# Feed-forward stages of a fused transformer kernel: output bias and parked rows added by GpSimd, shifted rows loaded two groups ahead, statistics taken two groups ahead

## The reference

```python
def _layer(x, wqkv, qs, ksc, wo, lg, lb, w1, b1, w2, b2):
    h = shift_token(x)          # second half of the channels comes from the token before
    ...                         # local attention with 8 heads of 64
    x = x + o @ wo
    h = shift_token(x)
    mu = h.mean(-1, keepdims=True)
    var = h.var(-1, keepdims=True)
    h = (h - mu) / jnp.sqrt(var + 1e-05) * lg + lb
    h = h @ w1 + b1
    a, g = jnp.split(h, 2, axis=-1)      # 341 and 341
    h = a * jax.nn.gelu(g, approximate=False)
    x = x + h @ w2 + b2
    return x
```

## Time and profile before

| what | value |
|---|---|
| median of the runs | 3533.75 us |
| the profiled execution's own time | 3536.04 us |
| its span, first to last instruction | 3534.4 us |
| mean granted TensorE clock | 0.947 of full speed |
| PE busy | 87% of the span |
| DVE busy | 76% |
| ACT busy | 46% |
| POOL busy | 24% |

### The profile page before, as it was taken

The page is one execution under the profiler, slowest core; times in us unless marked ns, Lnnn a source line. Parts: engine busy times, 40 slices in busy tenths (PEclk is TensorE's granted clock), DMA queues, the critical chain, the costliest instruction groups (busy, mean ns, idle before and its releaser), DMA issues. The chain is left out here.

```text
span 3534.4 us, 95348 instructions
## 1 busy us (share of the span) xinstructions
PE 3087.3 (87%) x34384; PEld 2089.7 (59%) x34384; DVE 2690.6 (76%) x5841; ACT 1625.1 (46%) x2545; POOL 839.8 (24%) x892
## 2 busy tenths in 40 slices
PE   4998769998999979999899668898979788888787
PEld 2666656665666656666566446666655456656545
DVE  5887767886777767766688779999956689989655
ACT  2665115664333335543466435555532355555422
POOL 1000000000000000001000156666611466666311
PEclk9999559998999989999899879999999999999999
DMA  4110001110000021110111100000001000000022
GB/s 137 30 29 20 0 5 31 29 29 4 0 0 0 0 44 38 41 22 1 28 27 29 62 13 7 9 9 8 4 19 27 13 11 10 9 11 8 19 65 59
DMA packets 193061, 80.16 MB, mean 23 GB/s; under 512 B 179124, under 2 KB 181864, under 8 KB 192232
## 3 DMA queue, kind: packets, MB, share of 16 engines
q1 hardware_dynamic: 191592, 73.25, 8.9%
q0 software_dynamic: 1280, 4.20, 0.3%
HBM read 35.58 MB, written 8.39 MB: 12 GB/s over the span
## 5 line engine op out<-in xcount | busy, mean ns | idle before, releaser
L770 ACT ACTIVATE probs_t<-ps_pt 128x1024 f32<-128x1024 f32 x256 | 262.2, 1024 | 384.8 <-PE ps_pt L884 384.8
L632 DVE TENSOR_REDUCE row_max<-ps_s 128x16 f32<-128x1024 f32 x256 | 313.2, 1224 | 135.2 <-PE ps_s L873 132.5
L1961 POOL TENSOR_TENSOR kblk<-kblk 128x1024 f32<-128x1024 f32 x128 | 301.6, 2356 | 199.1 <-DVE kblk L2002 199.1
L637 DVE TENSOR_TENSOR probs<-ps_s,row_max 128x1024 f32<-128x1024 f32 x256 | 312.1, 1219 | 11.7
L906 PE MATMUL ps_o<-v,probs_t 128*64 128x18 f32 x8192 | 285.4, 212 | 5.4 <-issue 5.2
L616 POOL TENSOR_TENSOR x<-x,out_bias_L 128x512 f32 (+1 forms) x32 | 40.7, 1272 | 1030.3 <-DVE x_norm L426 520.8
L906 PEld LDWEIGHTS ps_o<-v,probs_t 128*64 128x64 f32 x8192 | 260.1, 138 | 40.3 <-issue 19.0
L884 PE MATMUL ps_pt<-ident,probs 128*128 128x128 f32 x2048 | 277.1, 278 | 2.9 <-ACT probs L765 2.9
L873 PE MATMUL ps_s<-kblk,q_t 64*64 64x512 f32 x2048 | 273.5, 607 | 7.0 <-issue 6.9
L765 ACT ACTIVATE probs<-probs 128x1024 f32<-128x1024 f32 x256 | 269.6, 1053 | 16.6 <-DVE probs L637 15.1
L1979 POOL TENSOR_TENSOR kblk<-kblk,small_d 128x1024 f32<-128x1024 f32 x128 | 243.6, 1903 | 50.7 <-POOL small_d L1971 50.7
(11 more groups left out here) (307 smaller groups left out, 6930.7 us busy)
## 6 DMA issues: line engine op xcount, KB each, us to landing
ci<-in_ctx_t SPq DMA_DIRECT2D x64, 256.0 KB, 3.0
kblk<-k_t SPq DMA_DIRECT2D x768, 16.0 KB
ci<-x SPq DMA_DIRECT2D x64, 128.0 KB
ci<-x SPq DMA_DIRECT2D x128, 63.0 KB
x<-in_x_in SPq DMA_DIRECT2D x4, 1024.0 KB, 8.0
mask<-in_mask_l SPq DMA_DIRECT2D x64, 64.0 KB, 2.5
kblk<-ci SPq DMA_DIRECT2D x256, 16.0 KB
out<-x SPq DMA_DIRECT2D x1, 4096.0 KB, 11.1
```

Of the source, the lines that this page charges most:

```text
L632: dve.tensor_reduce(row_max[u % 2][:, :], scores_of(u), AX, ALU.max).then_inc(max_ready.sem, 1)
L637: dve.tensor_tensor(probs[u % 2][:, :, :], scores_of(u), row_max[u % 2][:, :].unsqueeze(2).broadcast_to([P, HEADS, S]), ALU.subtract).then ...
L770: act.activation(probs_t[:, :, :], ps_pt[:, :, :].rearrange("p a (r t) -> p (a r) t", t=P), ACT.Copy).then_inc(pt_ready.sem, 1)
L1961: pool.tensor_tensor(a, a, b_, ALU.add).then_inc(rotated.sem, 1)
```

## The change

The bias matmuls are taken out of PE's program. `b_dn` is loaded as full rows, and POOL adds it to the rows of x (`add_bias`) once the shifted copies of these rows are there; in layer 1 POOL adds the parked rows too, in place of DVE. SP loads the shifted rows two groups ahead, in `local_attention` too, and fetches the parked rows under a semaphore of their own (`fetched`). DVE takes the statistics of group g+2 between gates 0 and 1 of group g and their variances behind gate 2, and normalises group g+1 ahead of gate 0. The loops are `run_pipeline`, which was there before: it calls the body from group -2 on, and `has(g)` says whether there is such a group.

```diff
-                           (b_dn[l][0:1, :], w["b_dn"][l]), (ln_gb[l][:, :], w["ln"][l])]
+                           (b_dn[l][:, :], w["b_dn"][l]), (ln_gb[l][:, :], w["ln"][l])]
...
-                sp.wait_ge(zeroed.sem, len(row_bias) + 3 + DEPTH)
+                sp.wait_ge(zeroed.sem, len(row_bias) + 3)
...
-                for l in range(DEPTH):
-                    dve.memset(b_dn[l][:, :], 0.0).then_inc(zeroed.sem, 1)
...
-                if last:
-                    sp.dma_start(parked[par], out[:, rows, :]).then_inc(shift_loaded.sem, 16)
-
-            def body(g, par, ahead):
-                if ahead:
+
+            def fetch(g, par):
+                sp.dma_start(parked[par], out[:, bass.ds(g * GT, GT), :]).then_inc(fetched.sem, 16)
+
+            def body(g, par):
+                if not has(g + 2):
+                    return
+                if has(g):
                     sp.wait_ge(xt_in_psum.sem, xt_in_psum.at(g, 1))
                     sp.sem_inc(sp_turn.sem, 1)
-                    load(g + 1, 1 - par)
+                wait_past(sp, shift_loaded, g + 1, shift_loaded.per if has(g + 1) else 0)
+                sp.sem_inc(sp_turn.sem, 1)
+                load(g + 2, par)
+                if last:
+                    if has(g):
+                        sp.wait_ge(biased.sem, biased.at(g, biased.per))
+                        sp.sem_inc(sp_turn.sem, 1)
+                    wait_past(sp, fetched, g + 1, 16 if has(g + 1) else 0)
+                    sp.sem_inc(sp_turn.sem, 1)
+                    fetch(g + 2, par)
 
             sp.wait_ge(first_rows.sem, 4)
-            load(0, 0)
-            run_groups(sp, body)
+            run_pipeline(sp, body, 2)
...
-            shift_loaded.opens(4 * 16 if last else 3 * 16)
+            shift_loaded.opens(3 * 16)
+            fetched.opens(16 if last else 0)
+            biased.opens(2 if last else 1)
...
-                                pe.matmul(ps_o[:, u * P:(u + 1) * P], wide[c][0:m, u * P:(u + 1) * P],
-                                          w_dn[l][0:m, c, :], start=c == 0 and u == 0, stop=False,
-                                          skip_group_check=True)
-                        for u in range(GT):
-                            last = pe.matmul(ps_o[:, u * P:(u + 1) * P], ones[:, :], b_dn[l][:, :], start=False,
-                                             stop=True, skip_group_check=True)
+                                last = pe.matmul(ps_o[:, u * P:(u + 1) * P], wide[c][0:m, u * P:(u + 1) * P],
+                                                 w_dn[l][0:m, c, :], start=c == 0 and u == 0, stop=c == NC - 1,
+                                                 skip_group_check=True)
                         last.then_inc(y_done.sem, 1)
...
-                    def body(g, par, ahead):
-                        if ahead:
-                            root(pool, g + 1)
+                    def add_bias(g, par):
+                        if has(g + 1):
+                            pool.wait_ge(x_norm_ready.sem, x_norm_ready.at(g + 1, GT))
+                            pool.sem_inc(pool_turn.sem, 1)
+                        pool.wait_ge(shift_loaded.sem, shift_loaded.at(g, 48))
+                        pool.sem_inc(pool_turn.sem, 1)
+                        rows = x[:, bass.ds(g * GT, GT), :]
+                        pool.tensor_tensor(rows, rows, b_dn[l][:, :].unsqueeze(1).broadcast_to([P, GT, P]), ALU.add)\
+                            .then_inc(biased.sem, 1)
                         if last:
+                            pool.wait_ge(biased.sem, biased.at(g, 1))
+                            pool.sem_inc(pool_turn.sem, 1)
+                            pool.wait_ge(fetched.sem, fetched.at(g, 16))
+                            pool.sem_inc(pool_turn.sem, 1)
+                            pool.tensor_tensor(rows, rows, parked[par], ALU.add).then_inc(biased.sem, 1)
+
+                    def body(g, par):
+                        if has(g):
+                            add_bias(g, par)
+                        if has(g + 2):
+                            root(pool, g + 2)
+                        if last and has(g):
                             pool.wait_ge(added.sem, added.at(g, 1))
                             pool.sem_inc(pool_turn.sem, 1)
                             rows = bass.ds(g * GT, GT)
                             pool.dma_start(out[:, rows, :], x[:, rows, :]).then_inc(result_out.sem, 16)
 
-                    root(pool, 0)
-                    run_groups(pool, body)
+                    run_pipeline(pool, body, 2)
                     if last:
                         pool.wait_ge(result_out.sem, 16 * GROUPS)
 
                 @block.vector
                 def _(dve):
-                    def body(g, par, ahead):
-                        if ahead:
-                            dve.wait_ge(shift_loaded.sem, shift_loaded.at(g + 1, shift_loaded.per))
-                            norm_stats(dve, g + 1, hi[1 - par])
-                        flat = window_of(g)
-                        if last:
-                            dve.tensor_tensor(flat, flat, parked[par].rearrange("p u c -> p (u c)"), ALU.add)\
-                               .then_inc(unparked.sem, 1)
-                        for c, (at, m) in enumerate(HC):
-                            dve.wait_ge(a_in_psum.sem, a_in_psum.at(g, c + 1))
-                            dve.wait_ge(gelu_done.sem, gelu_done.at(g, c + 1))
-                            dve.wait_ge(y_done.sem, y_done.at(g, 0))
-                            dve.scalar_tensor_tensor(out=wide[c][0:m, :], in0=bank_a[c % 2][0:m, :],
-                                                     scalar=b_up1[l][0:m, c:c + 1], in1=wide[3 + c][0:m, :],
-                                                     op0=ALU.add, op1=ALU.mult).then_inc(gated.sem, 1)
-                            if ahead and c == 0:
-                                normalise(dve, g + 1, hi[1 - par])
-                        dve.wait_ge(y_done.sem, y_done.at(g, 1))
-                        if last:
-                            dve.wait_ge(unparked.sem, unparked.at(g, 1))
-                        dve.tensor_tensor(flat, ps_o[:, :], flat, ALU.add).then_inc(added.sem, 1)
-
-                    dve.wait_ge(shift_loaded.sem, shift_loaded.at(0, shift_loaded.per))
-                    norm_stats(dve, 0, hi[0])
-                    normalise(dve, 0, hi[0])
-                    run_groups(dve, body)
+                    def gate(g, c):
+                        m = HC[c][1]
+                        dve.wait_ge(a_in_psum.sem, a_in_psum.at(g, c + 1))
+                        dve.wait_ge(gelu_done.sem, gelu_done.at(g, c + 1))
+                        dve.wait_ge(y_done.sem, y_done.at(g, 0))
+                        dve.scalar_tensor_tensor(out=wide[c][0:m, :], in0=bank_a[c % 2][0:m, :],
+                                                 scalar=b_up1[l][0:m, c:c + 1], in1=wide[3 + c][0:m, :],
+                                                 op0=ALU.add, op1=ALU.mult).then_inc(gated.sem, 1)
+
+                    def body(g, par):
+                        now, late = has(g), has(g + 2)
+                        if has(g + 1):
+                            normalise(dve, g + 1, hi[1 - par])
+                        if now:
+                            gate(g, 0)
+                        if late:
+                            dve.wait_ge(shift_loaded.sem, shift_loaded.at(g + 2, 48))
+                            for u in range(GT):
+                                tile_stats(dve, g + 2, u, hi[par])
+                        if now:
+                            for c in range(1, NC):
+                                gate(g, c)
+                        if late:
+                            variance(dve, g + 2)
+                        if now:
+                            dve.wait_ge(y_done.sem, y_done.at(g, 1))
+                            dve.wait_ge(biased.sem, biased.at(g, biased.per))
+                            flat = window_of(g)
+                            dve.tensor_tensor(flat, ps_o[:, :], flat, ALU.add).then_inc(added.sem, 1)
+
+                    run_pipeline(dve, body, 2)
...
-        "dn": chunks(a["L3_ffn_w2"]), "b_dn": a["L3_ffn_b2"].reshape(DEPTH, 1, P),
+        "dn": chunks(a["L3_ffn_w2"]), "b_dn": np.broadcast_to(a["L3_ffn_b2"].reshape(DEPTH, 1, P), (DEPTH, P, P)),
```

More of the change, by code:

```diff
@@ L54 @@
 GROUP_SIGNALS = """
-gated_v qk_copied p_scaled bias_added a_in_psum added blended bn_done c_loaded chain damped exp_ready expo_ready g_in_psum gated
+gated_v biased fetched qk_copied p_scaled bias_added a_in_psum added blended bn_done c_loaded chain damped exp_ready expo_ready g_in_psum gated
 gates_in_psum gates_ready gates_t_ready gelu_done hidden_in_psum k_in_psum k_placed
@@ L60 @@
 route_in_psum router_copied scored shift_loaded shifted sig silu_done squared summed carried
-sums_ready times_up top_ready turned unit unparked v_copied v_done v_even v_in_psum v_odd var_ready
```

(16 more changed lines are left out.)

## The result

The changed kernel took 3454.97 us, the median of four runs (3452.07 to 3456.42), against 3532.48 us before on the same chip: a ratio of 0.978, 95% interval 0.9763 to 0.9797. That is 77.5 us less, and 3459 us was forecast. The profiled execution took 3454.24 us, with a span of 3452.6.

The account below looks back on a forecast made before the run. PE's own work plus waits for DVE, and in layer 1 for a transfer, bound the feed-forward; 23.8 us from layer 0 and 51.9 from layer 1 made 75.7 us, giving 3459 us, range 3449 to 3474.

Parts of the forecast that it names:

- The forecast case (A): Feed-forward groups: gate 0 just late for chunk 2, period 8.59 us in both layers, 3459 us in all; chance 58%.
- Step (1), the bias: PE's bias matmuls in the feed-forward: removing them saves 0.87 us a group, all on PE's path, 32 groups.
- Step (3), root: POOL's root, moved behind gate 2's variances: ready 1.0 us before Newton; lateness beyond that would lengthen the period.
- Step (4), the adds: POOL's adds, one a group in layer 0, two in layer 1: 1.272 us each, 3 us of cover before the final add.
- Step (5), the loads: Layer 1's shift loads behind the parked-row fetch: cover 1.4 us, another 1.0 at root, so layer 0's period.
- Step (6), the ends: First groups gain 2.7 us in layer 0, 4.5 in layer 1; last groups 0.87 each; layer 1's first statistics 1.08.
- Rival C: Layer 1: POOL's store holds x_norm, up to 0.76 us in each of 15 groups, 3465 to 3470 us; chance 15%.
- Rival B: Feed-forward groups: gate 0 isn't late for chunk 2, period 8.28 us, 8.7 less, 3450 us; chance 12%.
- Rivals D and E: Layer 1's loads late, 13 us more, 3472 us, 10%; or POOL becomes the ring and the kernel is slower, 3%.

Follow-up runs that it names:

- e2: The changed kernel with the bias matmuls back on PE and without POOL's bias add: 3483.14 us, ratio 0.9864.
- e3: The kernel before with only the bias moved from PE to POOL, loads and DVE's order as they were: 3531.03 us, ratio 1.0001.
- e6: The changed kernel with gate 0 ahead of Newton and x_norm, the parked rows' fetch left ahead of the shift loads: 3449.98 us, ratio 0.9768.
- e8: The changed kernel with two more POOL adds a group in layer 1, their output read by nobody: 3462.73 us, ratio 0.9806.
- e7: The changed kernel with one more POOL add a group in layer 1, its output read by nobody: 3453.85 us, ratio 0.9782.
- e1: The changed kernel run again with no edit: 3454.7 us, ratio 0.9783.
- e4: The changed kernel with gate 0 ahead of Newton and x_norm, and the parked rows fetched behind the shift loads: 3446.37 us, ratio 0.976.
- e5: The changed kernel with the old order on DVE and POOL's root; loads two groups ahead and bias on POOL stay: 3471.02 us, ratio 0.983.
- e9: The changed kernel with DVE's and POOL's old order and the bias back on PE, loads still two groups ahead: 3502.74 us, ratio 0.9926.
- e10: The changed kernel without POOL's wait for x_norm ahead of the bias add: 3476.3 us, ratio 0.9852.

## Why the prediction was right

- *The forecast case (A).* Gate 0 at T + 2.84 in layer 0 and T + 2.95 in layer 1 (forecast 2.86), chunk 2 just behind it, period 8.53 and 8.64 (8.59). The 0.1 between the layers is in the final add, which starts at T + 0.33 and T + 0.43.
- *Step (1), the bias.* The size was right in the changed kernel (e2: 0.90 and 0.81 a group), the reason was not whole. It was taken to be on PE's path in the kernel before. There it stood beside a ring of the same length: transposes, shift loads of 4.1, statistics, x_norm. The idle time in the earlier trace rows was read rightly, but a wait of zero doesn't say that there is no second limit at zero; that the statistics followed at T + 0.94 had two causes. The change took both limits away, so the sum came out. As far as this step goes that was luck: the prediction doesn't name the loads as a limit in layer 0, and by its words the bias alone would have gained 28 us, where e3 gained nothing.
- *Step (3), root.* It starts at T + 7.4, Newton in the next group isn't held, as forecast.
- *Step (4), the adds.* 1.266 and 1.27 us, the price of the earlier trace rows for the same shape. They end at T + 6.35 in layer 1, not 5.8: POOL starts 0.45 behind the end of x_norm and takes 0.35 between the two adds.
- *Step (5), the loads.* The cover was put at 1.4 us. The fetch starts at T + 6.67 (forecast 5.8) and the shift loads at T + 7.80 (6.7). In the run with two more adds such loads are used 4.18 after their start, so by this estimate they land here about 3373.8, and the statistics start at 3374.07: some 0.3 is left of the 1.4. It was enough. e6 and e8 show what happens beyond it. One more add still cost nothing, though the statistics waited about 1 us for the loads (e7): gate 1 and root have room behind the statistics. The prediction had such a second cover, of 1.0, at root.
- *Step (6), the ends.* Layer 1's first group gained 4.2 (4.5), layer 0's only 1.1 (2.7). The first four blocks of PE ran at a mean granted clock of 0.54 there, against 0.71 before. In e6, where it was 0.70, the same group took 9.83, which would be 2.7. So this term hangs on where the clock rises, and the 1.1 lies below the 1.44 that the prediction had as its lower end.
- *Rival C* is out: POOL's store (3363.65, 0.60) and x_norm (3363.74, 1.11) overlap in each group of layer 1, and no x_norm of the 60 recorded there took over 0.351. *Rival B* isn't the changed kernel, but its period, 8.28, is what the run with gate 0 first has. *Rivals D and E* would have needed late loads or a late root, as e8 makes them with two more adds; in the changed kernel no statistics of DVE's wait for a transfer and no Newton step for root.
- *Outside the stages.* Local attention of layer 0 took 551.1 us before, and 548.1 to 548.3 in the changed kernel, e1, e4, e5 and e7, but 550.9 to 551.0 in e2, e6 and e8, which have the same local attention with the same loads. (It was 551.1 in e3, with the old loads, and 550.0 and 548.5 in e9 and e10.) So the 3 us are not the work of the changed loads. They go with the clock: over its first part (2046 to 2090 us) the mean granted clock was 0.80 to 0.83 in every kernel in which the stretch took 548, and 0.72 to 0.75 in every one in which it took 550 or 551. Where it took 548, the first group of the feed-forward that follows took about 11.4 us, and in e6 and e8 9.8: half is given back. What moves the clock's steps from one program to the next wasn't tried. In layer 1 the same stretch was 573.4 before, 569.1 in the changed kernel and 568 to 572 in the other runs; beyond the 1.1 at the start of the feed-forward, its 3.2 us of gain in the profiled pair stay open.

## What to carry to other kernels

Before a matmul's cost is taken off a period, list every chain that ends at that point, with those that end at the same moment: a wait of zero can have two causes, and only a change that takes both away is worth anything. A transfer or an add that is hidden should be placed with its cover in microseconds, and with all that is queued behind it on its engine: here the fetch that nobody waited for held the loads that everybody needed. And where POOL and DVE both work from SBUF, the order in which they start is worth a wait of its own.

## What the runs showed of the hardware

A POOL add over 128x512 holds a later x_norm of DVE's, or a DVE step with two inputs in SBUF, until the add ends. Four x_norm grew from 1.11 to 2.40 us around an add of 1.27. In the run with gate 0 first and the fetch behind, a step over 4 elements with two inputs met the second add:

```profile
3397.19 1.26 POOL L2174 TENSOR_TENSOR x<-x,k_t 128x512 f32 x1 [0.35 <-POOL x L2167]
3397.21 1.26 DVE L369 TENSOR_TENSOR mean_gap<-bn 128x4 f32<-128x4 f32 x1
3398.40 0.15 DVE L371 TENSOR_TENSOR dev<-bn 128x4 f32<-128x4 f32 x1
```

It took 1.26 us where the next takes 0.15, and the period didn't change, because nothing waited. The other way round it holds too: in layer 1 of e3 POOL's root starts 0.2 behind DVE's add of the parked rows (0.69, two inputs in SBUF) and takes 1.36 us in place of 1.02. Statistics, with one input in SBUF, and gates, with one in SBUF and one in PSUM, ran over the adds at their usual 0.86 and 0.74. The Trainium skill, SBUF — State Buffer, section "Who interferes with whom", states this as an exclusive lock for the whole instruction, for a DVE instruction in a 2-port mode, or with two SBUF inputs beside a GpSimd instruction that reads SBUF, and whoever starts first has it. The runs agree, with the numbers above; which of the two kinds x_norm is, no trace says. That POOL's store left x_norm alone (0.60 and 1.11 side by side) is what the changed kernel's trace adds.
